# A folded weight chain: top coefficients as four spread rows, and spreads placed between the fold's steps

## What is computed

```python
kv = ctx * ctx                                   # k and v are both the context
r_t = 0.9 * r_(t-1) + kv_t                       # scan over the 512 positions
x = x + layernorm(x) * r
h = layernorm(x) @ W_exp + b_exp                 # 512 -> 2048
h = butterfly(h, up_weights)                     # 11 stages, s = 2**stage
h = gelu(h + up_bias)
h = butterfly(h, down_weights)
x = x + h @ W_con + b_con + down_bias            # 2048 -> 512

# butterfly, stage with stride s: y as (nb, 2, s), w = weights[stage] as (nb, s, 2, 2)
na  = w[..., 0, 0] * a + w[..., 0, 1] * b
nb2 = w[..., 1, 0] * a + w[..., 1, 1] * b
```

## Time and profile before

| What | us |
|---|---|
| median of three runs | 2804.66 |
| the profiled execution | 2804.95 |
| its span, from the first to the last instruction | 2803.1 |
| TensorE matmul busy | 2749.5 (98%) |
| VectorE busy | 2126.2 (76%) |
| ScalarE busy | 1149.5 (41%) |
| GpSimd busy | 396.2 (14%) |

### The profile page before, as it was taken

The page is one execution under the profiler, slowest core; times in us unless marked ns, Lnnn a source line. Parts: engine busy times, 40 slices in busy tenths (PEclk is TensorE's granted clock), DMA queues, the critical chain, the costliest instruction groups (busy, mean ns, idle before and its releaser), DMA issues.

```text
span 2803.1 us, 35216 instructions
## 1 busy us (share of the span) xinstructions
PE 2749.5 (98%) x12281; PEld 2272.2 (81%) x12281; DVE 2126.2 (76%) x3558; ACT 1149.5 (41%) x1700; POOL 396.2 (14%) x568
## 2 busy tenths in 40 slices
PE   8879999999999999999999999999999999999999
PEld 6748888888888888888888888888888888888887
DVE  7768777887877788787778878777887877788533
ACT  6753433434343343434334343433434343343432
POOL 4621111010111101011110201111020111102000
PEclk8889999999999999999999999999999999999999
DMA  8696575856757585665758567575857657585543
GB/s 212 174 336 191 170 211 155 250 164 201 204 167 214 154 251 164 203 204 166 216 158 242 165 203 203 166 221 157 239 165 209 197 167 224 153 243 163 181 150 99
DMA packets 293924, 540.44 MB, mean 193 GB/s; under 512 B 38718, under 2 KB 102366, under 8 KB 276854
## 3 DMA queue, kind: packets, MB, share of 16 engines
q1 hardware_dynamic: 287382, 534.80, 64.5%
q0 software_dynamic: 1520, 2.27, 0.4%
q10 hardware_dynamic: 4848, 1.13, 0.2%
HBM read 447.89 MB, written 56.62 MB: 180 GB/s over the span
## 4 chain that ended last, share of the span: by engine, by line
PE 94%; DMA 3%; DVE 1%; SPq 1%; ACT 1%; issue 0%; DVEq 0%; ACTq 0%
PE ps L1482 43%; PE ps L1500 25%; PE ps L1513 25%; DMA wcon<-in_L_ffn_W_con_dram 1%; DMA kv<-in_ctx_dram 1%; PE ps L1343 0%; PE ps L1391 0%; PE ps L1382 0%; SPq L450 0%; DMA w_products<-xop 0%; DVE w1r L1002 0%; DMA w_split<-w2s 0%; ACT Z L741 0%; PE ps L1562 0%; PE ps L1399 0%
## 5 line engine op out<-in xcount | busy, mean ns | idle before, releaser
L1482 PE MATMUL ps<-xop,w1r 128*128 128x512 f32 x5376 | 1365.7, 390 | 7.1 <-ACT st L858 4.8
L1482 PEld LDWEIGHTS ps<-xop,w1r 128*128 128x128 f32 x5376 | 1010.4, 188 | 218.9 <-DVE xop L1088 5.2
L1500 PE MATMUL ps<-w2r,ghi 128*128 128x512 f32 x2048 | 630.5, 389 | 0.0
L1513 PE MATMUL ps<-w2r,ghi 128*128 128x512 f32 x2032 | 626.1, 389 | 3.7 <-DVE x L1184 3.7
L858 ACT ACTIVATE st<-ps 128x512 f32<-128x512 f32 x384 | 229.7, 598 | 838.6 <-PE ps L1482 838.4
L1184 DVE TENSOR_TENSOR x<-ps,x 128x512 f32<-128x512 f32 x508 | 348.9, 687 | 280.4 <-PE ps L1513 277.8
L1513 PEld LDWEIGHTS ps<-w2r,ghi 128*128 128x128 f32 x2032 | 381.6, 188 | 83.3 <-DVE x L1184 4.1
L1500 PEld LDWEIGHTS ps<-w2r,ghi 128*128 128x128 f32 x2048 | 384.4, 188 | 79.8
L862 ACT ACTIVATE g<-g,gelu_bias 128x512 f32<-128x512 f32 x384 | 275.2, 717 | 368.7 <-DVE g L1202 368.7
L1202 DVE TENSOR_TENSOR g<-ps,st 128x512 f32<-128x512 f32 x384 | 262.8, 684 | 215.5 <-PE ps L1482 215.2
L1207 DVE TENSOR_TENSOR glo<-g,ghi 128x512 fp32r<-128x512 f32 x510 | 345.5, 698 | 79.6 <-ACT ghi L876 79.5
(11 more groups left out here) (138 smaller groups left out, 1651.3 us busy)
## 6 DMA issues: line engine op xcount, KB each, us to landing
w1r<-w_products SPq DMA_DIRECT2D x889, 256.0 KB, 3.3
w2r<-w_split SPq DMA_DIRECT2D x128, 1024.0 KB, 5.0
x<-in_x_dram SPq DMA_DIRECT2D x128, 256.0 KB, 7.0
raw<-kv SPq DMA_DIRECT2D x496, 64.0 KB, 2.3
out_dram<-x SPq DMA_DIRECT2D x120, 256.0 KB, 4.1
kv<-in_ctx_dram SPq DMA_DIRECT2D x64, 256.0 KB, 7.4
raw<-in_ctx_dram SPq DMA_DIRECT2D x64, 256.0 KB, 5.1
w_split<-w2s SPq DMA_DIRECT2D x12, 512.0 KB, 6.7
```

What stands on the lines that cost most here:

```text
L1482: last = nc.tensor.matmul(bank[:, :], w1r[:, slot, w, c * P:(c + 1) * P], xop[:, XPOS[m], v, c, :], start=(opens and i == 0), stop=(i == l ...
L1500: last = nc.tensor.matmul(ps_ya[j][:, :], g[:, p % 2, q, j * P:(j + 1) * P], w2r[:, p % 2, kk, w, :], start=(p == 0 and kk == 0 and i == 0 ...
L1513: last = nc.tensor.matmul(ps_yb[:, :], g[:, p % 2, q, j * P:(j + 1) * P], w2r[:, p % 2, kk, w, :], start=(kk == 0 and i == 0), stop=(kk == ...
```

## The change

The top coefficients of each chain are loaded as four rows of 1024 instead of a broadcast. They are split into a rounded part (`top_hi`) and a remainder (`top_lo`), spread by eight matmuls of TensorE, and multiplied out of PSUM in four pieces (`top_products`). The wide low stages lie as parts on partitions 0 and 32 of one operand, so that one matmul does both parts (6 matmuls instead of 12). Stages 0 and 1 are loaded as whole rows, laid out in `low_lanes` by three VectorE copies and spread by six matmuls of 16 columns. The spreads of the high and down chains, which stood behind `low_up` and `regroup`, now stand between the steps of `low_up` and `high_up`. The up coefficients are issued on ScalarE's queue, the first half of `W_con` is loaded early, and the steps of GpSimd and VectorE are reordered. The diff, cut to its core:

```diff
@@ -266,7 +277,7 @@
             for u in range(1, U):
                 body(u, u % 2, first=False, last=(u == U - 1))
 
...
         HIGH_PLACE = [(4, 448), (4, 384), (4, 256), (4, 0)]
         LOWS = LOW - 1
+
+
...
         def load_coefs(eng, weights, dn):
-            for stage in range(LOWS):
+            eng.dma_start(low_rows[dn], weights[0:len(WHOLE)].rearrange("s (k n) a b -> k s (n a b)", k=KH))\
+               .then_inc(low_loaded[dn], NX)
+            for stage in range(len(WHOLE), LOWS):
                 rows, off, n = src_place(stage)
                 src = weights[stage].rearrange("(k q l) a b -> q k (l a b)", k=KH, q=rows)
                 eng.dma_start(low_src[dn][0:rows, off:off + n].rearrange("q (k n) -> q k n", k=KH), src)\
                   .then_inc(low_loaded[dn], NX)
+        LOW_LOADS = 1 + LOWS - len(WHOLE)
...
         def load_top(eng, weights, dn):
-            eng.dma_start(top_src[dn], weights[LOW - 1].rearrange("m a b -> (m a b)").partition_broadcast(P))\
-              .then_inc(top_loaded[dn], NX)
+            eng.dma_start(top_src[dn][0:4], weights[LOW - 1].rearrange("(o n) a b -> o (n a b)", o=4))\
+               .then_inc(top_loaded[dn], NX)
 
...
-            load_wexp(0)
-            load_coefs(sp, up_w, 0)
-            load_top(sp, up_w, 0)
-            for q in range(1, 4):
+            for q in range(4):
...
             load_tokens(kv, 0, ctx_rows, 0, ctx_loaded[0])
+            load_high(sp, up_w, 0)
             load_tokens(xs[0], 0, x_rows, 0, x_loaded[0])
-            load_top(sp, down_w, 1)
-            load_high(sp, up_w, 0)
             load_tokens(xs[0], 1, x_rows, 1, x_loaded[1])
 
             wcon_src = w_con.rearrange("(k e r) d -> e k (r d)", e=E, r=R)
...
+            load_wcon(0)
             sp.wait_ge(fold_made, fold_at("low_up", KH - 1) + 1)
+            load_top(sp, down_w, 1)
             load_tokens(raw[:, 1, :, :], 0, ctx_rows, 1, ctx_loaded[1])
-            sp.wait_ge(top_picked, 4)
+            sp.wait_ge(coef_spread, spreads(1, LOWS - 1))
             load_wcon(1)
-            sp.wait_ge(coef_spread, spreads(1, LOWS - 1))
-            load_wcon(0)
...
             sp.wait_ge(xn_turned, J)
-            sp.wait_ge(low_matrix_ready, 2)
             move_xT(sp, 0, 0, xT_moved[0])
             move_xT(sp, 0, 1, xT_moved[0])
...
+            for stage in range(LOWS - 1, len(WHOLE) - 1, -1):
+                choose(stage)
+            pool.wait_ge(sel_zero, 2)
...
             load_coefs(pool, down_w, 1)
+            pool.wait_ge(coef_spread, LOWS)
+            nc.gpsimd.memset(parts_zero(1), 0.0).then_inc(parts_zeroed, 1)
             load_high(pool, down_w, 1)
+            pool.wait_ge(fold_made, fold_at("low_up", KH - 1) + 1)
+            nc.gpsimd.memset(top_parts[1][0:Q].bitcast(f32), 0.0).then_inc(top_zeroed, 1)
             nc.gpsimd.memset(neg_half[:, :], -0.5).then_inc(neg_ready, 1)
             nc.gpsimd.memset(eps[:, :], EPS).then_inc(neg_ready, 1)
...
             def first_moves(h):
-                if h == 0:
-                    pool.wait_ge(low_matrix_ready, 2)
                 pool.wait_ge(xn_turned, (h + 1) * J)
                 move_xT(pool, h, 2, first_moved[h])
...
             pool.wait_ge(neg_ready, 2)
+            high_matrix(0)
             rstd_rows(0)
             rstd_gated(0)
-            high_matrix(0)
             high_matrix(1)
             first_moves(0)
             rstd_rows(1)
             wait_kept(pool, "high_up", R - 1)
+            pool.wait_ge(low_matrix_ready, 2)
             weight_sums(0)
             weight_sums(1)
...
+            load_coefs(act, up_w, 0)
+            load_top(act, up_w, 0)
...
-            def pick(dn):
+            def top_hi(dn):
                 act.wait_ge(top_loaded[dn], NX)
-                if dn:
-                    act.wait_ge(fold_made, fold_at("low_up", KH - 1) + 1)
-                for bit in range(1 + dn):
-                    act.activation(*top_halves(dn, bit), ACT.Copy).then_inc(top_picked, 1)
+                act.wait_ge(top_zeroed, dn + 1)
+                act.activation(top_part(dn, 0), top_whole(dn), ACT.Copy).then_inc(coef_hi, 1)
...
             for k in range(KH):
-                if k == KH // 4:
-                    coefs_hi(0)
+                if k == KH // 2:
+                    for stage in PARTED:
+                        coefs_hi(0, stage)
+                    top_hi(0)
                     act.dma_start(bias_row[:, :], b_con.partition_broadcast(P)).then_inc(bias_loaded, NX)
                     act.dma_start(bias_tmp, down_bias.partition_broadcast(P)).then_inc(bias_loaded, NX)
-                    pick(0)
-                    coefs_hi(1)
+                if k == 12:
+                    square(0, 0)
                 fold_step("WT", k)
-            square(0, 0)
             for k in range(KH):
                 fold_step("low_up", k)
-            pick(1)
+                if k in (5, 7):
+                    coefs_hi(1, PARTED[k == 7])
+            top_hi(1)
...
+            nc.vector.memset(top_choice[0:Q], 0.0).then_inc(sel_zero, 1)
...
+            nc.vector.memset(parts_zero(0), 0.0).then_inc(parts_zeroed, 1)
+            nc.vector.memset(top_parts[0][0:Q].bitcast(f32), 0.0).then_inc(top_zeroed, 1)
...
+            def lane_rows(dn):
+                dve.wait_ge(low_loaded[dn], LOW_LOADS * NX)
+                if dn:
+                    dve.wait_ge(coef_spread, len(WHOLE))
+                for stage in WHOLE:
+                    n = 1 << stage
+                    src = low_rows[dn][:, stage, :].rearrange("k (q n b) -> k n q b", n=2 * n, b=2)
+                    to = low_lanes[:, 2 * n - 2:4 * n - 2, :].rearrange("k n (q b m) -> k n q b m", b=2, m=n)
+                    for m in range(n):
+                        nc.vector.tensor_copy(to[:, :, :, :, m], src).then_inc(lanes_ready, 1)
...
+            def top_lo(dn):
+                dve.wait_ge(coef_hi, dn * PARTS + PARTS)
+                nc.vector.tensor_tensor(out=top_part(dn, Q), in0=top_whole(dn), in1=top_part(dn, 0).bitcast(f32),
+                                        op=ALU.subtract).then_inc(coef_lo, 1)
...
-                path_products(dn, 0, LOWS, LOW_PLACE, half[:, :], flat(LX[:, dn, :, :]), KH,
-                              None if dn else pick_second)
...
+            def top_products(dn):
+                dve.wait_ge(path_product, spreads(dn, LOWS - 1))
+                dve.wait_ge(top_spread, dn + 1)
+                for c, bank in enumerate(TOP_PLACE[dn]):
+                    last = path_stage(nc.vector, flat(LX[:, dn, 4 * c:4 * c + 4, :]), half[:, 2 * c * P:2 * (c + 1) * P],
+                                      spread_view(ps[bank][:, :], 0, LOW - 1, KH // 4), LOW - 1)
+                last.then_inc(low_matrix_ready, 1)
...
             for k in range(KH // 4):
                 fold_step("WT", k)
+
+            dve.wait_ge(sel_ready, 2 * len(PARTED))
+            for lane in (0, Q):
+                nc.vector.tensor_copy(sel_parts[lane:lane + Q], sel[0:Q, PARTED[0]:LOWS]).then_inc(sel_rounded, 1)
+            dve.wait_ge(top_sel_ready, 2)
+            for lane in (0, Q):
+                nc.vector.tensor_copy(top_sel[lane:lane + Q], top_choice[0:Q]).then_inc(top_sel_ready, 1)
+            lane_rows(0)
             coefs_lo(0)
+            top_lo(0)
             low_products(0)
-            dve.wait_ge(path_product, LOWS)
-            dve.wait_ge(top_picked, 2)
-            top_stage(nc.vector, 0).then_inc(low_matrix_ready, 1)
             for k in range(KH // 4, KH):
                 fold_step("WT", k)
-            coefs_lo(1)
+            top_products(0)
             dve.wait_ge(const_ready, 2)
             dve.wait_ge(bias_loaded, 4 * NX)
             nc.vector.tensor_tensor(out=bias_row[:, :], in0=bias_row[:, :], in1=bias_tmp, op=ALU.add)\
                 .then_inc(bias_row_ready, 1)
             dve.wait_ge(bias_row_ready, 1)
-            for j in range(J):
-                scan_chunk(0, 0, j)
+            lane_rows(1)
+            scan_chunk(0, 0, 0)
+            scan_chunk(0, 0, 1)
+            scan_chunk(0, 0, 2)
+            coefs_lo(1)
+            scan_chunk(0, 0, 3)
+            high_products(0)
             stats1(0, 0, xs[0], range(J))
             gate(0, 0, xs[0], 0)
             gate(0, 0, xs[0], 1)
             gate(0, 0, xs[0], 2)
             gate(0, 0, xs[0], 3)
-            high_products(0)
             for j in range(J):
                 normalise(0, 0, xs[0], j)
+            top_lo(1)
             low_products(1)
-            dve.wait_ge(path_product, spreads(1, LOW - 2))
-            dve.wait_ge(top_picked, 4)
-            top_stage(nc.vector, 1).then_inc(low_matrix_ready, 1)
+            high_products(1)
             scan_chunk(1, 1, 0)
             scan_chunk(1, 1, 1)
-            high_products(1)
+            top_products(1)
             scan_chunk(1, 1, 2)
             scan_chunk(1, 1, 3)
...
+                def whole_spread(place, stage):
```

(38 more changed lines are left out.)

172 lines of the change are left out of this document (97 added, 75 removed).

## The result

The changed kernel takes **2826.55 us** (median of 6 runs, 2820.25 to 2827.63) against 2805.4 of the kernel before beside it: 1.0071 times as long, 95% interval 1.0058 to 1.0084. It is slower, as forecast, but by 21 us where 8 were forecast, and outside the range of 2799.5 to 2817.5. Its times lie in two groups: of ten runs in all, two took 2819 to 2820 us and eight 2825 to 2829. The first profile is of an execution of the small group (2820.25 us, span 2818.5), the second, of the same kernel, is of the large one (2827.85 us, span 2826.0). The mean granted clock of TensorE goes with the groups: 0.987 and 0.988 in the two executions, 0.982 to 0.984 in the eight.

A forecast was written before the change was run, and what follows sets the result against it. The fold before the loop was taken to bound the change, through `low_up`, GpSimd and VectorE's first gate: 10.1 us late, less 0.7, less 1.30 slack, +8.1 on 2804.95, 0.3 off for the median: 2812.8 us, range 2799.5 to 2817.5.

The forecast's parts named there:

- Start of `low_up`: In the fold, TensorE's `low_up` was to begin at 32.5 us, between 31 and 34.5; before, it began at 31.09.
- The wait for the square at 36.47: Inside `low_up`, the 2.46 us stand until the square let ScalarE go on was to vanish, the square coming earlier.
- Length of `low_up`: On TensorE, 16 steps at 0.92 us (14.7) plus spreads sum to 24.1 us, so `low_up` ends at 56.6.
- at double pace: In `low_up`, six parted spread matmuls cost 3.0 us at 0.5 each, 1.5 at double pace; 1.7 was taken.
- GpSimd: After `low_up`, clearing 1.0, `high_matrix` 3.8 and `rstd_rows` 1.36 us put the first gate at 62.8, 10.1 late.
- From the first gate to the second: On VectorE, savings and additions sum to -0.7 us, so the second group's first gate starts near 107.3 instead of 97.87.
- Earlier work of TensorE alone is worth nothing: In the fold, only when VectorE reaches its work at 113.94 counts; VectorE delays beyond 1.3 us move the loop.
- regroup late instead: Rival: second context asked for after `low_up` makes `regroup` 2 us late, hidden; alone 2807; chance 0.20 shared with hidden spreads.
- The slack at the end: At 113.94, VectorE's 1.30 us of slack against ScalarE is used up, so 9.4 us late becomes +8.1.
- The wait for `W_con` ahead of `high_dn`: In the fold's chain, this wait was to go through the early first half of `W_con`, but give nothing.
- a saving of 1.3 us: On VectorE behind the first gate, `high_products(0)` already done was to save 1.3 us, 1.14 and its first copy.

## Why the prediction was right, and where it was wrong

**Start of `low_up`: right.** 32.5 forecast, 32.10 and 30.86 in the two profiles. The wait for the square at 36.47 went.

**Length of `low_up`: the step that failed.** The prediction set 16 steps x 0.92 = 14.7 and 9.4 us of spreads, 24.1. It was 32.1 in the first profile and 37.1 in the second. Of the first one, by starts: five steps in line 5.0; seven single ones at 1.09, 7.6; two at 2.0, 4.0; the last two 3.5; 20.2 instead of 14.7. The spreads took 4.2 (high, 3.8 forecast), 3.1 (narrow, 2.9), 1.5 (the six small ones, 1.0) and 3.2 (parted, 1.7); 11.9 instead of 9.4. So of the 8.0 us missing in the first profile, 3.9 are four steps at the low clock, 1.2 are seven steps that took 1.09 instead of 0.92, 0.4 is a low clock at the very start of `low_up`, and 2.5 are spreads. In the second profile eight steps ran at the low clock, for 15.8 us instead of 7.4. The working took each price from the row in which that work stood, and put them together as if the clock belonged to neither. The profile of the kernel before spoke against it (its windows above): the parted spreads ran at the low clock there, and the prediction even halved them "at double pace" for `low_up`, where they then ran at 0.50 and cost 3.2 us, near the 3.0 that it had as their full price.

**GpSimd: right.** 0.94, 3.67 and 1.36 us (1.0, 3.8 and 1.36 forecast), 6.1 from `low_up`'s end to the gate against 6.2. VectorE was ready at 55.2 (54.2 forecast) and waited 15.19 instead of 7, since `low_up` ended 7.6 us later than forecast. From the first gate to the second it was 46.8 us, where the working had 44.5; in them are the 3.73 us of waiting for the high spreads, which it did not have.

**"Earlier work of TensorE alone is worth nothing": wrong.** Adding the missing 8 us of `low_up` to the prediction gives 2821.1, next to the profiled 2820.25; but this agreement is luck, since with the first gate 13 us earlier the time did not fall. The path that the prediction followed, GpSimd's reciprocal and the first gate, was not the only late one; TensorE's chain was late by as much. The rival "regroup late instead" named it and put it at 2 us, hidden, because it hung on the same length. A reason that holds for the kernel before (VectorE has 1.30 us of slack and all else is early) is no reason for the changed one, in which TensorE's `low_up` took 8 to 13 us more than its sum.

**The slack at the end: not settled.** The second gate's delay and the time of the same execution can be compared in the thirteen profiles other than that of the kernel before. From 101.61 (3.7 us late, no slower) over 107.55 (9.7 late, 4.7 slower) to 133.12 (35.3 late, 33.4 slower), the time is 0.7 to 5.1 us less late than the gate, 2.9 in the mean. So a late second gate is paid nearly in full, as the prediction had it. Whether its slack of 1.3 us was too small can't be told: the two executions whose gates came at 105.75 and 105.69 are 4.3 us apart in time (2807.7 and 2812.03). The wait for `W_con` ahead of `high_dn` did go: that step now waits for ScalarE only.

**The wait that was not priced.** The prediction let `high_products(0)` move ahead of the first gate as a saving of 1.3 us behind it. With the spreads back, it waits 4.2 us for TensorE in front of all gates; moving it behind them gave 5.8 us (2809.61 to 2803.83; 5.0 by the ratios), most of what the spreads had left of the loss. In the changed kernel itself this wait is not there: its `high_products(0)` starts at 50.99 without one, and VectorE then waits for GpSimd. So the 14 us of the spreads and these 5 to 6 us are not two shares of one profile; the second shows only once the first is gone.

## What to carry to other kernels

Matmuls that are moved into a gap-free stretch bring their pace with them: price the *neighbours* too, from rows at both levels of the clock, not from the row in which they ran before. When one chain is delayed, look for a second that hangs on the same event before crediting the fix of the first; here GpSimd's reciprocal first, alone, gave nothing, the second context early, alone, at most 4 us, and the time came back with four edits together (spreads out, context ahead of `W_con`, reciprocal first, gates first). Which of the four it can do without was not run in full. A matmul that is moved forward in a list also brings its wait with it: the same interleaving in the kernel before made TensorE stand 10.50 us for a load that the old place had covered. And a large load put early on a queue delays what is issued behind it (4.7 us to landing became 14.7), whether or not that costs time.
